# An adjacency GNN in two residual blocks: the beginning of the kernel rearranged

## The reference

```python
u = einsum('bid,bjd->bij', h, h) / sqrt(384)
a = softmax(u); delta = a * adj
attn = delta / (sum(delta, -1) + 1e-10)
ctx = (attn * upper) @ (h @ wl.T + bl) + diag(attn) * (h @ ws.T + bs) + (attn * lower) @ (h @ wr.T + br)
h = relu(layernorm(ctx) * gamma + beta)
```

## Time and profile before

| what | us |
|---|---|
| median of three runs | 1221.1 |
| the profiled execution, whole | 1221.88 |
| its span | 1220.1 |
| TensorE busy (matmuls) | 1203.8 |
| VectorE busy | 1060.7 |
| ScalarE busy | 983.3 |
| GpSimd busy | 313.0 |

### The profile page before, as it was taken

The page is one execution under the profiler, slowest core; times in us unless marked ns, Lnnn a source line. Parts: engine busy times, 40 slices in busy tenths (PEclk is TensorE's granted clock), DMA queues, the critical chain, the costliest instruction groups (busy, mean ns, idle before and its releaser), DMA issues.

```text
span 1220.1 us, 26540 instructions
## 1 busy us (share of the span) xinstructions
PE 1203.8 (99%) x7067; PEld 1197.5 (98%) x7067; DVE 1060.7 (87%) x2863; ACT 983.3 (81%) x2673; POOL 313.0 (26%) x421
## 2 busy tenths in 40 slices
PE   8899999999999999999999999999999999999997
PEld 7899999999999999999999999999999999999997
DVE  6789898988888888888888888998989899998976
ACT  6677777777778788888888888888888888888874
POOL 2223222232222121222212121223333232323221
PEclk9899999999999999999999999999999999999999
DMA  5434343433232323343333323323232323332321
GB/s 182 128 96 126 108 127 98 128 92 117 89 107 72 96 87 117 104 125 114 111 116 104 108 85 105 112 85 96 97 107 97 107 95 96 103 97 98 99 94 55
DMA packets 112955, 127.57 MB, mean 105 GB/s; under 512 B 11104, under 2 KB 100192, under 8 KB 112864
## 3 DMA queue, kind: packets, MB, share of 16 engines
q1 hardware_dynamic: 112864, 126.50, 32.9%
HBM read 76.91 MB, written 49.55 MB: 104 GB/s over the span
## 4 chain that ended last, share of the span: by engine, by line
PE 96%; ACT 1%; DVE 1%; DMA 1%; issue 1%; SPq 0%; POOL 0%; POOLq 0%; DVEq 0%; ACTq 0%
PE left_bank L474 24%; PE context_bank L474 24%; PE right_bank L474 24%; PE context_bank L505 17%; PE score_bank L450 5%; DMA rows<-weights 1%; PE edge_bank L458 0%; PE edge_bank L464 0%; DMA nodes<-squares 0%; ACT weight L696 0%; DVE weight L906 0%; ACT nodes L579 0%; SPq L365 0%; DVE context L963 0%; ACT side_parts L643 0%
## 5 line engine op out<-in xcount | busy, mean ns | idle before, releaser
L474 PE MATMUL left_bank<-weight,node_t 128*128 128x384 f32 x1728 | 337.8, 338 | 0.0
L474 PE MATMUL context_bank<-weight,node_t 128*128 128x384 f32 x1728 | 332.6, 337 | 4.6 <-ACT context_bank L653 4.6
L474 PE MATMUL right_bank<-weight,node_t 128*128 128x384 f32 x1728 | 333.9, 338 | 0.3 <-DVE weight L906 0.3
L474 PEld LDWEIGHTS context_bank<-weight,node_t 128*128 128x128 f32 x1728 | 303.5, 189 | 5.2 <-ACT context_bank L653 5.0
L474 PEld LDWEIGHTS left_bank<-weight,node_t 128*128 128x128 f32 x1728 | 303.6, 188 | 0.0
L474 PEld LDWEIGHTS right_bank<-weight,node_t 128*128 128x128 f32 x1728 | 299.6, 188 | 0.7 <-issue 0.7
L505 PE MATMUL context_bank<-side_parts,attn_t 128*128 128x386 f32 x1152 | 240.0, 343 | 2.0 <-issue 1.9
L505 PEld LDWEIGHTS context_bank<-side_parts,attn_t 128*128 128x128 f32 x1152 | 199.5, 189 | 3.5 <-issue 3.3
L643 ACT ACTIVATE side_parts<-right_bank 128x384 fp32r<-128x384 f32 x192 | 94.5, 492 | 128.3 <-PE context_bank L505 128.3
L1143 POOL TENSOR_TENSOR rstd<-spread,scalars 128x2 f32<-128x2 f32 x95 | 68.4, 720 | 500.4 <-DVE spread L941 500.4
L816 DVE TENSOR_TENSOR node_t<-nodes,node_t 128x768 fp32r<-128x768 f32 x94 | 145.4, 1547 | 9.5 <-ACT node_t L584 9.1
(11 more groups left out here) (88 smaller groups left out, 1593.4 us busy)
## 6 DMA issues: line engine op xcount, KB each, us to landing
squares<-turned SPq DMA_DIRECT2D x94, 384.0 KB, 2.7
nodes<-squares SPq DMA_DIRECT2D x376, 96.0 KB, 2.2
rows<-x SPq DMA_DIRECT2D x64, 384.0 KB, 4.1
out<-rows SPq DMA_DIRECT2D x31, 384.0 KB, 2.6
adj_in<-adj SPq DMA_DIRECT2D x96, 64.0 KB, 1.9
piece<-weights SPq DMA_DIRECT2D x18, 192.0 KB, 2.5
rows<-weights SPq DMA_DIRECT2D x3, 576.0 KB, 7.8
vector_rows<-vectors SPq DMA_DIRECT2D x3, 384.0 KB, 3.6
```

The lines of the kernel that those rows point to most:

```text
L474: mm = nc.tensor.matmul(bank[:, 0:D], node_t[:, s.parity, k, c, a], weight[:, s.phase % 2, w, c, b], start=False, stop=(c, a) == (CH - 1, ...
```

## The change

The edits are all in the beginning, steps 0 and 1:

- SyncE: the rows of pair 0 come in two transfers, tile by tile, with a semaphore for the first. Identity, right chunk 0, right bias, right chunks 1 and 2, left weights, rows of pair 1, left bias, self weights follow, then the rest as before.
- Pair 2 is transposed by TensorE, in step 1 behind the left projection of tile 0. It is not written to the scratch or read back. Pair 3 is the first that is, so waits that count turned or written pairs count one less.
- The right projection of the very first tile waits only for that tile's split (`first_split`), and for the chunks one by one.
- Three filler matmuls become six, and six become five.
- ScalarE's `first_step` fills pair 2 later and no longer fills pair 3; a new `second_step` is step 1's order. The same on VectorE. GpSimd's order is as it was.

```diff
@@ SyncE, body
+                if first:
+                    return
+                if isinstance(s.n, int) and s.n == 1:
+                    sp.wait_ge(nodes_turned, 1)
+                    write_squares(after)
                 if third.exists():
-                    sp.wait_ge(nodes_turned, third.n - 1)
+                    sp.wait_ge(nodes_turned, third.n - 2)
@@ SyncE, beginning
-            load_x(Step(0, 0, 0))
+            sp.dma_start(rows[:, 0], x_pairs[0, :, 0]).then_inc(first_x_in, 16)
+            sp.dma_start(rows[:, 1], x_pairs[0, :, 1]).then_inc(x_in[0], 16)
             sp.dma_start(context[:, 0, 0:P], identity).then_inc(identity_in, 16)
+            load_first(RIGHT, (0,), first_chunk_in)
+            load_first_bias(RIGHT)
+            load_first(RIGHT, (1, 2), first_in[RIGHT])
+            load_first(LEFT, (0, 1, 2), first_in[LEFT])
             load_x(Step(0, 0, 1))
-            for w in (RIGHT, LEFT):
-                load_first_bias(w)
-                load_first(w)
+            load_first_bias(LEFT)
+            load_first(SELF, (0, 1, 2), first_in[SELF])
             load_adj(Step(0, 0, 0))
...
-            load_first(SELF)
...
-            sp.wait_ge(nodes_turned, 1)
-            write_squares(Step(0, 1, 0))
@@ TensorE
                 project_side(s, 0, LEFT)
+                if isinstance(s.n, int) and s.n == 1:
+                    transpose_first(nxt)
                 project_self(s, 0)
...
-            keep_busy(3)
+            keep_busy(6)
...
-            keep_busy(6)
+            keep_busy(5)
@@ ScalarE, first_step (from the split of pair 1's nodes)
                 split_first_nodes(nxt)
                 split_edges(s)
-                fill_source(second, 0)
-                fill_source(second, 1)
                 scale_self(s, 0)
                 seed_self(s, 1)
                 copy_cross(nxt)
                 seed_side(nxt, 0, RIGHT)
                 split_side(s, 1, RIGHT)
                 split_side(s, 1, LEFT)
-                fill_source(third, 0)
-                fill_source(third, 1)
+                fill_source(second, 0)
+                fill_source(second, 1)
                 scale_self(s, 1)
                 seed_side(nxt, 0, LEFT)
                 exponentials(nxt)
+            def second_step(s):
+                nxt, second, third = s.ahead(1), s.ahead(2), s.ahead(3)
+                split_side(s, 0, RIGHT)
+                seed_self(s, 0)
+                seed_side(s, 1, RIGHT)
+                split_edges(s)
+                split_side(s, 0, LEFT)
+                split_first_nodes(nxt)
+                fill_source(second, 0)
+                fill_source(second, 1)
+                scale_self(s, 0)
+                copy_cross(nxt)
+                seed_side(s, 1, LEFT)
+                fill_source(third, 0)
+                fill_source(third, 1)
+                split_side(s, 1, RIGHT)
+                seed_self(s, 1)
+                exponentials(nxt)
+                seed_side(nxt, 0, RIGHT)
+                split_side(s, 1, LEFT)
+                seed_side(nxt, 0, LEFT)
+                scale_self(s, 1)
@@ ScalarE, beginning
             act.wait_ge(banks_open, 1)
+            split_first(RIGHT, (0,))
             seed_side(start, 0, RIGHT)
             split_first_nodes(start)
-            split_first(RIGHT)
+            split_first(RIGHT, (1, 2))
             seed_side(start, 0, LEFT)
+            split_first(LEFT)
             fill_source(start.ahead(1), 0)
-            split_first(LEFT)
@@ VectorE, first_step (from the LO edges)
                 gather_stats(third)
-                turn_nodes(second)
-                input_shift(third)
+                sum_scores(nxt)
+                context_stats(s, 0)
+                denominator(s, 0)
                 split_side(s, 1, RIGHT)
                 split_side(s, 1, LEFT)
-                sum_scores(nxt)
                 add_cross(nxt)
-                context_stats(s, 0)
-                denominator(s, 0)
-                turn_nodes(third)
+                input_shift(third)
                 gather_moments(s, 0)
                 mask_edges(nxt)
                 centre(s, 0)
                 gather_stats(fourth)
                 input_shift(fourth)
+            def second_step(s):
+                diagonal(s)
+                context_stats(prev, 1)
+                denominator(prev, 1)
+                split_side(s, 0, RIGHT)
+                gather_moments(prev, 1)
+                squared_denominator(prev)
+                spreads(prev)
+                split_side(s, 0, LEFT)
+                split_edges(s)
+                split_first_nodes(nxt)
+                centre(prev, 1)
+                turn_nodes(second)
+                norm(prev, 0)
+                sum_scores(nxt)
+                add_cross(nxt)
+                input_stats(fourth, 0)
+                input_stats(fourth, 1)
+                split_side(s, 1, RIGHT)
+                gather_input(fourth, 0)
+                gather_input(fourth, 1)
+                turn_nodes(third)
+                context_stats(s, 0)
...
+                input_shift(fourth)
+                centre(s, 0)
+                split_side(s, 1, LEFT)
@@ VectorE, beginning
             input_shift(start)
+            split_first(RIGHT, (0,))
+            split_first_nodes(start)
+            split_first(RIGHT, (1, 2))
             gather_stats(start.ahead(1))
-            split_first_nodes(start)
+            split_first(LEFT)
             input_shift(start.ahead(1))
-            split_first(RIGHT)
-            split_first(LEFT)
```

More of the change, by code:

```diff
@@ L487, in project_side @@
             def project_side(s, k, side, within=None):
-                pe.wait_ge(node_hi, s.n + 1)
-                pe.wait_ge(node_lo, s.n + 1)
+                if isinstance(s.n, int) and (s.n, k, side) == (0, 0, RIGHT):
+                    pe.wait_ge(first_split, 1)
+                else:
+                    pe.wait_ge(node_hi, s.n + 1)
+                    pe.wait_ge(node_lo, s.n + 1)
                 pe.wait_ge(side_seeded[side], s.tile(k) + 1)
@@ L567, in fill_source @@
             def fill_source(s, k):
-                if isinstance(s.n, int) and s.n in (1, 2):
+                if isinstance(s.n, int) and s.n in (1, 2, 3):
                     act.wait_ge(first_moved, 2 * s.n)
-                elif isinstance(s.n, int) and s.n == 3:
+                elif isinstance(s.n, int) and s.n == 4:
                     act.wait_ge(nodes_turned, 1)
-                elif not isinstance(s.n, int) or s.n > 3:
+                elif not isinstance(s.n, int) or s.n > 4:
                     act.wait_ge(node_lo, s.n - 1)
@@ L690, in square, with split_first @@
                                      accum_out=moments[:, k, 1:2]).then_inc(squared, 1)
[L692 to L696, removed]
+            def split_first(w, chunks=range(CH)):
+                for i in chunks:
+                    act.wait_ge(first_chunk_in if (w, i) == (RIGHT, 0) else first_in[w], 16)
+                    nc.scalar.activation(piece_part(0, w * CH + i, HI), first_raw[:, w * CH + i], ACT.Copy).then_inc(first_hi[w], 1)
             def first_step(s):
-                nxt, second, third = s.ahead(1), s.ahead(2), s.ahead(3)
+                nxt, second = s.ahead(1), s.ahead(2)
                 split_side(s, 0, RIGHT)
@@ L727, in body @@
                     return first_step(s)
+                if isinstance(s.n, int) and s.n == 1:
+                    return second_step(s)
                 prev, nxt, third = s.ahead(-1), s.ahead(1), s.ahead(3)
@@ L789, in input_stats @@
             def input_stats(s, k):
-                if s.phase == 0:
+                if isinstance(s.n, int) and (s.n, k) == (0, 0):
+                    dve.wait_ge(first_x_in, 16)
+                elif s.phase == 0:
                     dve.wait_ge(x_in[s.parity], 16 * (s.half + 1))
@@ L900, in split_piece, with split_first @@
                                                piece_part(phase, i, HI).bitcast(F32), ALU.add, ALU.subtract).then_inc(piece_lo, 1)
-            def split_first(w):
-                for i in range(CH):
+            def split_first(w, chunks=range(CH)):
+                for i in chunks:
                     dve.wait_ge(first_hi[w], i + 1)
@@ L1007, in first_step @@
                 input_shift(fourth)
+            def second_step(s):
+                prev, nxt, second, third, fourth = s.ahead(-1), s.ahead(1), s.ahead(2), s.ahead(3), s.ahead(4)
+                diagonal(s)
[20 more added lines that the diff above has]
+                context_stats(s, 0)
+                denominator(s, 0)
+                mask_edges(nxt)
+                norm(prev, 1)
+                gather_moments(s, 0)
+                input_shift(fourth)
+                centre(s, 0)
+                split_side(s, 1, LEFT)
             def body(s):
```

17 lines of the change are left out of this document (10 added, 7 removed).

## The result

The changed kernel takes 1226.97 us (median of five runs, 1226.46 to 1227.44) against 1221.24 us of the kernel before beside it (1220.22 to 1223.57). The ratio is 1.0041, with a 95% interval of 1.003 to 1.0052, so the change made the kernel slower, by 0.4%. The profiled execution took 1226.46 us, its span is 1224.7 us, and that is 4.6 us over the span before. The difference of the medians is 1.1 us more than that; executions without a profile have no trace, and where this 1.1 us lies is open.

A forecast was written before the change was run, and what follows sets the result against it. TensorE is full from 42 us on, so only its waits and half clock before that count. The terms 1.8 - 1.0 + 1.5 + 1.0 = +3.3 us gave a forecast of 1224.4 us, range 1221.3 to 1227.0.

The forecast's parts named there:

- rival C: Same places as the forecast: transfers 1 us late or low clock longer, +5.5 us, 1226.6 us and above; 8%.
- Part 1: Opening: left bias and pair 1's rows, moved last, delay the cross block and pair 1's scores, +1.8 us.
- Parts 2 and 3: Steps 0 and 1: earlier weighing, but a 6.0 us gap replaces 4.65 before pair 2's scores; together -1.0 us.
- Part 4: Behind step 1's gap: clock at half for 5.7 us from the restart at pair 2's scores, +1.5 us.
- my low end: Clock behind step 1's gap: low stretch only as long in all as before (6.9 us), +0.9 us.
- half clock for over 5 us behind it: Sign to look for behind the TensorE wait at pair 2's scores: clock at half for over 5 us.
- Part 5: Step 2's self projection: waits for pair 3's nodes coming through DRAM, +1.0 us (0.5 to 1.4).
- Rival A: Step 1: gap and its half clock vanish, as if VectorE did not stand at pair 4's shift; 1216.2 us; 10%.
- Rival B: Opening: bias and rows land early, pair 1's scores only 0.3 us late, rest as forecast; 1222.9 us; 22%.

The follow-up runs named there:

- e7: Changed kernel with four filler matmuls behind pair 0's scores and four more ahead of the cross block in the first left projection; median 1225.01 us, ratio 1.0025.
- e1: Changed kernel with VectorE's input shift of pair 4 moved from step 0 to step 1, behind the LO split of pair 2's nodes; median 1220.04 us, ratio 0.9992.
- e5: Changed kernel with e1's move of the shift and e2's opening of the kernel before; median 1216.96 us, ratio 0.9959.
- e9: e5 with VectorE's step 1 reordered: pair 2's nodes before edges, pair 4's statistics later, tile 1's left LO part earlier; median 1216.56 us, ratio 0.9951.
- e2: Changed kernel with the whole opening (transfers, split orders, fillers) of the kernel before; median 1223.85 us, ratio 1.0018.
- e8: Changed kernel with pair 1's rows and the left bias issued ahead of the left weights; median 1224.93 us, ratio 1.0023.
- e3: Kernel before with only the changed kernel's opening (transfers, chunk by chunk splits, fillers); median 1223.1 us, ratio 1.0017.
- e4: Changed kernel with four more filler matmuls on TensorE behind the scores of pair 0; median 1226.76 us.
- e10: e9 with pair 0's rows in two transfers, tile by tile, the first statistics waiting for the first alone; median 1217.87 us, ratio 0.9957.

## Why the prediction was right, point by point

It named the right sign and the right places, and it was too low. The measured 1226.97 lies 0.03 us inside a range that ended at 1227.0; that is luck, for two of the five executions (1227.01 and 1227.44) lie outside. It is outside the forecast's own part of the range (1223.0 to 1226.0, given 60%) and among the times of rival C (1226.6 and above, given 8%). C's reason was later transfers or a longer low clock in the same place; what came instead was a second low stretch in a place to which the prediction gave no price. The sum was 3.3 us, and the profiled difference is 4.6. By its own terms:

1. *Part 1, the first transfers, +1.8.* Measured +3.7 (t0 25.50). The mechanism is the one named: the left bias and pair 1's rows are last of the same set of bytes; the bias was used at 12.76 where I had 12.4, the statistics began at 11.76 (11.9). The cross block was packed at 17.41 (17.0) and turned 2.2 us later than before. This part was mis-sized by 0.4 us only, less than the 0.95 by which equal openings differ. The left weights landed at 10.7, well ahead of the bias. What I left out is the clock: I wrote of TensorE's waits in the opening and gave them no price, although the change made them longer. They cost 1.5 us, by e7. That is the largest error of the sum. Two smaller ones stayed hidden: the first sources came 0.8 us sooner, not 0.5, and the five fillers took 1.41 us, not 2.1, for I had read their length from rows at half rate.
2. *Parts 2 and 3, steps 0 and 1, -1.0.* Measured -0.8: t0 to the scores of pair 2 is 16.08 us against 16.0 predicted, the weighing 0.97 behind t0 against 0.95. The gap is 5.71 us (6.0). e1 shows its cause as predicted, by taking away just that.
3. *Part 4, the clock behind the gap, +1.5.* Measured +0.7: the lag behind the kernel before is 2.9 us at the scores of pair 2 and 3.6 at the left projection of tile 1 (46.96 against 43.36 before). The clock was low from 38.8 to 45.7 us, 6.8 in all and 4.1 of it behind the restart; before it was low from 34.5 to 41.4, 6.8 too. So my low end (+0.9, a stretch as long in all as before) was nearly right and the term wrong, for I had counted from the restart. The sign "half clock for over 5 us behind it" failed with it.
4. *Part 5, pair 3's nodes, +1.0.* Measured: 0.84 by the idle row, and 1.0 in lag (55.30 against 50.68 is 4.6, from 3.6). It stays when the other losses are gone: e5 and e9 wait there 0.75 and 0.65 us.

Rival A (the gap goes, with t0 1 us late, 1216.2) needed the edit that e1 makes and the change does not; with the changed kernel's opening e1 takes 1220.0, and only with the old opening too, in e5, is it 1217.0. Rival B, an opening that is 0.3 us late, is nearly e2's (t0 22.16), made by undoing the opening; e8's t0 is 22.79, 1.0 late. The forecast's 1224.4 is 2.6 us below the median. About half of this is in the traces (4.6 measured, 3.3 summed: +1.9 in the opening, +0.2 in steps 0 and 1, -0.8 in the clock behind the gap); the other half is how the profiled executions stand to the medians, 0.8 above mine of before and 0.5 below that of the changed kernel.

## What to carry to other kernels

Where engines work in a written order, follow each moved instruction to what waits for it through the other engines' single buffers: here a fill moved behind new work held a tiny shift on another engine, and a whole step was queued behind the shift; moving that one instruction was worth 5.6 us. In the three orders of the same transfers tried here the last one was in at about the same time (12.4, 12.7 and 12.0 us), so put last what its consumer needs last in its own order. An idle place of 1 to 2 us on TensorE in an opening is to be priced with the clock that it may cost (1.5 us here), not only with its length. And where the clock falls in some executions only, look at the mean clock of all of them before a gain of 1 to 2 us is put down to an edit: e8's trace shows 3.2 us, its median 2.0.

## What was not expected of the hardware

The granted clock fell to half in the opening although no idle stretch of TensorE was longer than 2.5 us: at 14.9 us in the changed kernel (idle 2.05 ahead of it), at 16.4 us in e1 (2.45 and 1.74), at 18.1 in e3 (1.53 and 1.74), at about 18.5 in e4 (1.06 and 1.74), at 11.5 in e10 (2.07). In e9 it fell at 8.6, while TensorE was running its fillers, 1.0 us behind an idle stretch of 2.04. It stayed at 1.00 in the opening of e7 (1.50 and 0.82) and in the traced execution of e8 (1.01 and 1.75). So idle time of this length made a fall possible, not certain, and what decides between the two stayed open.

The kernel before has idled 1.88 us at 5.7 without a fall in its granted clock, but that is no sign of safety. Its matmuls had half rate already, and the clock's column does not show it: the column reads 1.00 from the start (the earlier trace rows has two places), while three transposes take what they take at half clock (0.84 in e1 at 21.82) and not the 0.49 of the same kernel at 17.58.

```profile
7.55 0.87 PE L439 MATMUL edge_bank<-ident_r,nodes 128*128 128x128 f32 x3 [1.88 <-ACT nodes L579]
```

The same holds for its six fillers at 8.72, with 0.42 us each. In e5 the transposes take 0.88 us there, and in e9, which has the same program up to step 1, 0.52. So how early TensorE gets its full rate differs between executions of one program. In the first 12 us read it from the lengths of matmuls, not from the clock's column.
